# Window and context attention on one Trainium2 core: consecutive context scores, a key projection behind the shift's transpose, five row transfers issued by ScalarE

## What is computed

```python
x = x + attn(layernorm(x), w_qkv, w_out)          # causal window of 128 keys + the first 16 keys, per sequence
x = x + xattn(layernorm(x), ctx, mask, Wq..bo)    # every token against the 64 context rows of its sequence
x = x + ffn(layernorm(x), ...)                    # attention over the batch, then 8 experts, one chosen per token
```

## Time and profile before

| | |
|---|---|
| time, median of 3 runs | 1140.19 us (1139.51 to 1141.94) |
| profiled execution: time / span | 1137.37 us / 1135.6 us |
| PE busy | 94% |
| DVE busy | 64% |
| ACT / POOL busy | 42% / 44% |
| granted PE clock, mean | 0.995 |

### The profile page before, as it was taken

How to read it: one execution, slowest core, us unless ns; L and a number is a source line. 1 busy time by engine, 2 the same in 40 slices (tenths; PEclk the granted TensorE clock), 3 DMA queues, 4 the chain that set the end, 5 groups by cost and what they waited for, 6 DMA issues and landing times. The chain is left out here.

```text
span 1135.6 us, 28867 instructions
## 1 busy us (share of the span) xinstructions
PE 1064.7 (94%) x9846; PEld 706.5 (62%) x9847; DVE 724.5 (64%) x2088; ACT 476.8 (42%) x869; POOL 497.0 (44%) x744
## 2 busy tenths in 40 slices
PE   9999899999999999999989889999989999999996
PEld 3546456455464464555645446666657999999963
DVE  4655776767757857767572654777774556665656
ACT  5435545454544545454535224333303333333342
POOL 3325424425245245253342221455554655555555
PEclk9999999999999999999999999999989999999999
DMA  7282573753735645727458225635313111111110
GB/s 223 77 217 74 155 192 100 190 152 113 208 88 152 166 123 155 183 76 206 118 137 217 64 76 170 204 113 199 121 39 113 57 56 52 54 53 52 54 37 9
DMA packets 143723, 137.53 MB, mean 121 GB/s; under 512 B 31640, under 2 KB 136990, under 8 KB 143520
## 3 DMA queue, kind: packets, MB, share of 16 engines
q1 hardware_dynamic: 137824, 123.72, 39.0%
q0 software_dynamic: 4992, 12.66, 3.3%
q10 hardware_dynamic: 832, 0.16, 0.1%
HBM read 48.50 MB, written 50.43 MB: 87 GB/s over the span
## 5 line engine op out<-in xcount | busy, mean ns | idle before, releaser
L980 ACT ACTIVATE probs<-ps_ab 128x512 f32<-128x512 f32 (+2 forms) x352 | 175.0, 540 | 86.0 <-PE ps_ab L1301 36.6
L600 POOL TENSOR_SCALAR_AFFINE_SELECT probs<-probs 128x512 f32<-128x512 f32 x128 | 83.4, 652 | 257.9 <-ACT probs L980 253.6
L3110 PE MATMUL ps_ab<-e_yT,e_w_now 128*128 128x128 f32 x1024 | 119.7, 275 | 0.1
L3110 PEld LDWEIGHTS ps_ab<-e_yT,e_w_now 128*128 128x128 f32 x1024 | 116.9, 192 | 0.4 <-ACT e_yT L3011 0.4
L3121 PE MATMUL ps_c<-keep_w,e_hT 128*128 x512 | 115.9, 379 | 0.0
L3121 PEld LDWEIGHTS ps_c<-keep_w,e_hT 128*128 128x128 f32 x512 | 94.8, 190 | 12.4 <-issue 0.8
L721 DVE CUSTOM_DVE_ANT_0 ps_ab<-ps_ab,mask_qk 128x256 f32<-128x256 f32 x224 | 89.3, 450 | 14.8 <-PE ps_ab L1271 14.6
L1271 PE MATMUL ps_ab<-k_rows,q_rows 96*128 96x256 bf16 (+1 forms) x512 | 84.5, 260 | 6.2 <-DVE top_prefix L707 2.9
L715 DVE TENSOR_REDUCE top<-ps_ab 128x2 f32<-128x512 f32 (+1 forms) x112 | 74.1, 683 | 25.2 <-PE ps_ab L1271 23.5
L1863 ACT ACTIVATE e_w_now<-keep_w 128x1024 f32 x64 | 64.1, 1049 | 30.4 <-DVE m_rows_upto_all L2455 20.4
L1301 PE MATMUL ps_ab<-q_rows,k_rows 98*128 98x256 bf16 (+1 forms) x512 | 75.5, 260 | 0.2
(11 more groups left out here) (290 smaller groups left out, 2189.1 us busy)
## 6 DMA issues: line engine op xcount, KB each, us to landing
sorted_rows<-filler SPq DMA_DIRECT2D x8, 4290.0 KB, 18.5
q_rows<-parts SPq DMA_DIRECT2D x96, 128.0 KB, 2.4
k_rows<-parts SPq DMA_DIRECT2D x96, 128.0 KB, 2.4
q_rows<-q_parts SPq DMA_DIRECT2D x96, 128.0 KB, 2.4
keep_w<-in_e_w SPq DMA_DIRECT2D x16, 512.0 KB, 4.7
keep_w<-in_e_w SPq DMA_DIRECT2D x8, 1024.0 KB, 8.0
e_row<-sorted_rows SPq DMA_DIRECT2D x32, 130.0 KB, 2.1
x_in<-in_x SPq DMA_DIRECT2D x8, 512.0 KB, 3.8
```

Of the source, the lines that this page charges most:

```text
L600: nc.gpsimd.affine_select(own, own, [[0, TILES], [1, P]], ALU.is_ge, keep_zero, base=0, channel_multiplier=-1).then_inc(probs_cut.sem, 1)
L980: nc.scalar.activation(probs[:, user % 2, lo:lo + width], ps_exp[:, f % 2, 0:width], ACT.Exp).then_inc(exp_done.sem, 1)
L3110: mm = nc.tensor.matmul(ps_h[s][:, f // 4, (f % 4) * P:(f % 4 + 1) * P], w1_now[:, s, k, f * P:(f + 1) * P], yT[:, s, k * P:(k + 1) * P], ...
```

## The change

Five things. (1) In full and last iterations, the first two late scores are issued right behind the heads' transposes, ahead of the transposes of xn. (2) The first context score stands ahead of shiftB's transpose, and the eight context scores follow each other without the key projection k1 between them; the last value step of group 1 comes behind shiftB's transpose; shifted steps (2,0) and (2,1) are put among the last context scores. (3) k1 is computed in one piece behind shift2's transpose and one more early score; with it go its entry in the bank table, its high and middle part on ACT, its rest on DVE, its low part on POOL. (4) ACT instead of SP issues five of the twelve row transfers of tile 0 (the query side's high and middle part). (5) On ACT, shiftB's copy and its two DMAs come ahead of the sums of group 1.

```diff
-         "q1", "shiftB", "k1", "s1", "shiftT2", "s2", "shiftA", "ctxT", "k2", "v2", "out2_0", "out2_1", "v0", "v1"]
+         "q1", "shiftB", "s1", "shiftT2", "k1", "s2", "shiftA", "ctxT", "k2", "v2", "out2_0", "out2_1", "v0", "v1"]
@@ SP, stack_front
+                            if tile == 0 and side == 0 and part < 2 and not (isinstance(n, int) and n == -1):
+                                continue
@@ POOL, iteration
                     if front:
-                        low_parts(n, range(2, 4))
+                        low_parts(n, (2,))
                     cut_group(n, 2)
+                    if front:
+                        low_parts(n, (3,))
                     cut_group(n, 3)
@@ DVE, iteration
                     if cross:
-                        context_maxima(n, range(TILES))
-                    if front:
-                        split_rest(n, (3,))
-                    if cross:
-                        context_maxima(n, range(TILES, TILES + 2))
+                        context_maxima(n, range(TILES + 2))
                     normalise_heads(n, 1)
                     if cross:
                         context_maxima(n, range(TILES + 2, CROSS_MAX))
                         context_shift(n)
-                    if front:
+                    if front and cross:
+                        early_maxima(n, range(3))
+                        split_rest(n, (3,))
+                        early_maxima(n, range(3, 13))
+                    elif front:
+                        split_rest(n, (3,))
                         early_maxima(n, range(13))
@@ ACT
+                def stack_queries(n):
+
+                    act.wait_ge(exp_full.sem, exp_full.count(n, exp_window(n, 1) + 9))
+                    for part, sig in enumerate((part_hi, part_mid)):
+                        act.wait_ge(sig.sem, sig.next(n, 1))
+                        for row in rows_of(part, 0):
+                            act.dma_start(q_rows[row:SPLIT_ROWS:PARTS, 0:8, :], parts[:, part, 0, :]).then_inc(rows_loaded[0].sem, 16)
...
                     if front:
+                        stack_queries(n)
                         high_part(n, 2)
-                    group_sums(n, 1)
-                    if front:
-                        middle_part(n, 2)
                     shift_rows(n, "shiftB", shiftT[1], shiftT_ready)
...
+                    group_sums(n, 1)
                     if front:
+                        middle_part(n, 2)
+                    if front and not cross:
                         high_part(n, 3)
                         middle_part(n, 3)
                     probs_claim(n, user_window(n, 2))
                     head_exps(n, 2, 0)
+                    if front:
+                        head_exps(n, 2, 1)
                     if cross:
                         shift_rows(n, "shiftT2", shiftT2, shiftT2_ready)
-                    for j in range(1, GROUP + 1):
+                    if front and cross:
+                        high_part(n, 3)
+                        head_exps(n, 2, 2)
+                        head_exps(n, 2, 3)
+                        middle_part(n, 3)
+                    for j in range((4 if cross else 2) if front else 1, GROUP + 1):
                         head_exps(n, 2, j)
@@ PE, iteration
                     if cross:
                         heads_transposes(n)
+                        late_scores(2)
...
                     window_shifted(n, 0, 3)
-                    late_scores(2)
+                    if not cross:
+                        late_scores(2)
...
-                    for j in range(2, GROUP + 1):
+                    for j in range(2, GROUP):
                         window_values(n, 1, j)
                         late_scores(1)
+                    if cross:
+                        context_scores(n, 0, (0,))
                     shift_transposes(n, "shiftB", shift[1], shift_ready, shift_ready.count(n, 2))
-                    if cross:
-                        context_scores(n, 0, range(2))
-                    if front:
-                        queries_or_keys(n, 3, (0,))
-                    if cross:
-                        context_scores(n, 0, (2,))
-                    if front:
-                        queries_or_keys(n, 3, (1,))
-                    if cross:
-                        context_scores(n, 0, (3,))
-                        context_scores(n, 1, range(2))
+                    window_values(n, 1, GROUP)
+                    if cross:
+                        context_scores(n, 0, (1, 2, 3))
+                        context_scores(n, 1, (0,))
                     sums_transposes(n, 1)
-                    if cross:
-                        context_scores(n, 1, range(2, TILES))
+                    if last:
+                        context_scores(n, 1, (1, 2, 3))
+                        return
+                    if cross:
+                        context_scores(n, 1, (1,))
+                        window_shifted(n, 2, 0)
+                        context_scores(n, 1, (2, 3))
+                        window_shifted(n, 2, 1)
+                        early_scores(1)
+                        shift_transposes(n, "shiftT2", shift2, shift2_ready, shift2_ready.count(n, 1))
+                        early_scores(1)
+                        queries_or_keys(n, 3)
+                        window_shifted(n, 2, 2)
+                        early_scores(1)
                     else:
+                        queries_or_keys(n, 3)
                         keep_warm(ps_out[:, 1, :], 6)
```

11 lines of the change are left out of this document (4 added, 7 removed).

## The result

The changed kernel takes 1146.77 us (median of 8 runs, 1145.28 to 1152.73), the kernel before 1141.13 beside it (8 runs, 1136.12 to 1144.09): a ratio of 1.0064, 95% interval 1.0047 to 1.0081. By the ratio it is slower by 7.3 us, by the medians by 5.6, where 1136.7 (faster) was forecast; it lies outside the forecast range of 1131.5 to 1141.5. The profiled execution took 1145.28 with a span of 1143.6.

The account below looks back on a forecast made before the run. TensorE, 94% busy, was taken to lose time in short holes, with VectorE setting the pace in stretch B. 6 x (0.58 + 0.20) + 0.55 - 1.7 = 3.5 us saved gave a median of 1136.7, range 1131.5 to 1141.5.

Parts of the forecast that it names:

- (1) Late scores: Start of an iteration: late scores fill TensorE's wait before xn's transposes; gain 0.58 us per iteration, bounds 0.41 to 0.6.
- (2) Stretch B: From group 1's value steps to the first shifted context step, VectorE-paced: reordering gains 0.20 us per iteration, bounds -0.4 to 0.9.
- (3) The five issues: ScalarE after the sums' copy: five DMA issues of 2.9 to 3.1 us hidden in 3.35 us idle, cost 0.
- Rival (b): First half's row transfers: DMA engines, not issues, are the limit, so nothing lands earlier; 1138.5 us, chance 0.17.
- (4) shiftB's rows: ScalarE's pair before shifted step (2,0): rows land at 441.7, wanted at 442.19; cover 0.5, cost 0.
- Rival (d): At shifted step (2,0): shiftB's rows land late, up to 5.2 us, TensorE waits 2.3; 1148.7 us, chance 0.13.
- (5) Key's rest and low part: On VectorE and GpSimd: SyncE wants the low part more than 25 us later; cost 0.
- (6) First sequence: Before the sums' transposes, no context scores there: TensorE waits for ScalarE's copy; cost 1.7 us once, bounds 0.5 to 2.2.
- (7) Last sequence: At out0, without xn transposes: the late scores' move fills an idle wait for ScalarE's copy; gain 0.55 us.

Follow-up runs that it names:

- eighth_transfers: The changed kernel with ScalarE's five row transfers cut to one head of eight each, same place and number: ratio 0.9988 to the kernel before.
- sp_issues_all: The changed kernel with SyncE again issuing all twelve row transfers of the first half, ScalarE none: ratio 1.0022 to the kernel before.
- combined_sp_issues: The changed kernel, first sequence as before, shifted step (2,0) behind the context scores, SyncE issuing all twelve row transfers: ratio 1.0076 to the kernel before.
- late_from_third: The kernel before with the late scores ahead of xn's transposes, but in the second sequence at their old place: ratio 0.9967 to the kernel before.

## Why the prediction was wrong

Its own steps, with the means of the traces where there are several.

- **(1) Late scores: right.** Forecast 0.58 per iteration, measured 0.62 in the trace after and 0.64 alone (77.24 to 76.60). Alone it is worth 0.9967, 3.8 us. Not foreseen was the second sequence, where the scores stand ahead of their rows.
- **(2) Stretch B: the mechanism right, the size nearly.** Forecast 0.20; with the landing out of the way the iteration is 76.48 instead of 76.60, so 0.12. In eighth_transfers shift2's transpose comes 8.83 us after the value steps (8.7 forecast, 10.23 before), the first shifted context step 14.90 (14.8 and 15.01), and the wait for exponentials at (2,3) is there, 0.30. The reordering itself is worth next to nothing.
- **(3) The five issues: hidden on ScalarE, as forecast,** though they take 3.3 to 3.7 us from the third sequence on (4.2 in the first two; all in the trace after) and not 2.9 to 3.1. SyncE's earlier end saves waits of 1.0 to 1.4 us at early score 0 (sp_issues_all and combined_sp_issues have them), as the same step said it would. Rival (b)'s condition, full engines, came true (1.13 to 1.14), but not its price: no kernel whose five rows ScalarE issues in this place beside SyncE's waits at early score 0 for rows from the third sequence on.
- **(4) shiftB's rows: this is the step that failed.** It took the landing from the trace of before, 2.3 us, for a kernel in which two engines issue at once, and so had a cover of 0.5 and cost 0: landing at 441.7 for a want at 442.19. Measured: 4.4 in the median, so that rows issued when forecast arrived 2 us later, and PE waited 1.2 to 1.5 us per sequence in the first trace, 2.0 in the second sequence. Each such wait cost 1.2. Rival (d) named the wait, and its break-even of about 4.0 fits (4.4 gave a small loss), but its 5.2 was too long, and its price of 2.3 per wait with it. Its reason, five transfers ahead in the same queue, isn't what the runs show: the pair is as late from a queue of its own. Its 5.2 came from the last sequence of before, where the engines are full (0.99); what made that one late was not asked. (d) got 0.13 because "the five should be through by 439", which counted issue times and not how full the engines were. I had worked that out for rival (b): 2.0 MB at 209 GB/s. The engines' share was compared with 1 for one issuer (0.79) and never added up for two. With two, SyncE's key rows slowed as well, from 2.4 to 4.2 us.
- **(5) Key's rest and low part: cost 0,** no row shows a wait for them.
- **(6) First sequence: the hole as described, its price too low.** Forecast 1.7, measured 3.9 in the trace and 4.2 in the mean. The hole was put at 1.85 (64.0 to 65.85) and is 2.51: the five issues, 4.16 us long there, stood in no term of it (without them it is 1.83), and the low clock behind it, 1.4 us, had no term either.
- **(7) Last sequence: more gain than forecast,** 1.0 in the mean for 0.55.

So (4)'s wait turned a gain of 0.76 per iteration into a loss of about 0.4. From the forecast -3.5 to the measured +6.8 of the attention part it is 10.3 us: 6.0 in the third to seventh sequences (five times 1.2), 2.3 in the second, 2.5 in the first, less 0.5 in the last.

What stays open: whether the instruction transfers of the loop's first pass are what makes SyncE's issues longer there and the rows of the first half late once. They come together in late_from_third and in the traces of before, and no run takes them apart. Nor does any run show why a wait of the same length sometimes brings the low clock and sometimes doesn't.

## What to carry to other kernels

Handing transfers to a second engine did more here than hide issue time: with two issuers the transfer engines' share went from 0.79 to 1.13, SyncE's key rows took 4.2 us to land instead of 2.4 and shiftB's pair 4.4 instead of 2.4. So every landing taken from the old trace has to be taken again, the small and urgent ones above all. Before moving a consumer of a small transfer forward, add up the share of the engines for all issuers in its window (0.79 with one was 1.13 with two). A long landing among short ones in the old trace is worth a look at the engines' share beside it: here 5.2 us at a share of 0.99 was the changed kernel's case in small. And of a change with several parts, time the parts alone: here one was worth 0.9967, one next to nothing, and one was good only if the consumer stayed late. Together, with the consumer late and the first sequence left as it was, they gave 0.9955, all at once as written 1.0064.
